# Two conditional residual layers: transposed operands from the host, a fused mask product, and layer 0 of batch b+1 ahead of layer 1 of batch b

## What is computed

```python
# per batch b of 8: x is 256x1024, mask 1024x1024 of 0/1, W0 and W1 1024x1024, A 1024x16, B 16x1024
y = x + (x @ W0.T + b0 + (x @ (2*mask[b] - 1)) * coeff[b])
z = y + (y @ W1.T + b1 + 2.0 * (y @ A[slot[b]]) @ B[slot[b]])
```

## Time and profile before

| what | us |
|---|---|
| device time, median of 3 runs | 426.68 |
| the three runs | 426.68, 426.79, 423.54 |
| span of the profiled execution | 421.9 |
| PE busy in it | 411.8 (98%) |
| DVE busy / ACT busy / POOL busy | 229.0 / 229.4 / 38.8 |
| first matmul of layer 0 | at 13.56 |
| first matmul of layer 0 of batch 1 | at 79.66 |
| last closing matmul's copy begins | at 419.07 |

### The profile page before, as it was taken

How to read it: one execution, slowest core, us unless ns; L and a number is a source line. 1 busy time by engine, 2 the same in 40 slices (tenths; PEclk the granted TensorE clock), 3 DMA queues, 4 the chain that set the end, 5 groups by cost and what they waited for, 6 DMA issues and landing times.

```text
span 421.9 us, 7924 instructions
## 1 busy us (share of the span) xinstructions
PE 411.8 (98%) x3034; PEld 408.3 (97%) x3034; DVE 229.0 (54%) x281; ACT 229.4 (54%) x371; POOL 38.8 (9%) x43
## 2 busy tenths in 40 slices
PE   6997999999999999999999999999999999999997
PEld 5897999999999999999999999999999999999996
DVE  1888786465536665374546755356653745365300
ACT  3775786664546465474547555363655735464311
POOL 1123530020000200020000200002000200002000
PEclk9999999999999999999999999999999999999999
DMA  7999735372146603292144712375142721440011
GB/s 227 341 332 322 254 153 197 105 230 101 50 151 178 251 5 139 74 309 101 50 149 128 246 55 61 138 230 198 49 125 93 260 99 50 149 132 0 2 50 51
DMA packets 34612, 61.56 MB, mean 146 GB/s; under 512 B 10652, under 2 KB 20004, under 8 KB 34598
## 3 DMA queue, kind: packets, MB, share of 16 engines
q1 hardware_dynamic: 31984, 52.96, 38.3%
q10 hardware_dynamic: 2614, 8.41, 5.6%
HBM read 52.97 MB, written 8.39 MB: 145 GB/s over the span
## 4 chain that ended last, share of the span: by engine, by line
PE 96%; DMA 1%; ACT 1%; issue 1%; POOL 0%; SPq 0%; ACTq 0%; POOLq 0%
PE y_ps L378 44%; PE z_ps L405 43%; PE z_ps L329 2%; PE z_ps L431 2%; PE t_ps L352 2%; DMA w_stage<-in_w 1%; PE y_ps L329 1%; PE z_ps L352 1%; PE y_ps L352 1%; ACT wc_hi L518 0%; PE y_ps L421 0%; PE y_ps L292 0%; ACT w_t L536 0%; PE t_ps L329 0%; POOL w_stage L247 0%
## 5 line engine op out<-in xcount | busy, mean ns | idle before, releaser
L378 PE MATMUL y_ps<-x_hi,wc_hi 128*128 128x256 f32 x512 | 143.0, 283 | 0.7 <-ACT wc_hi L518 0.7
L378 PE MATMUL y_ps<-x_lo,wc_hi 128*128 128x256 f32 x512 | 142.7, 283 | 0.0
L378 PE MATMUL y_ps<-x_hi,wc_lo 128*128 128x256 f32 x512 | 137.4, 284 | 0.0
L405 PE MATMUL z_ps<-w_hi,y_hi 128*128 128x344 f32 (+1 forms) x384 | 125.4, 327 | 0.0
L405 PE MATMUL z_ps<-w_lo,y_hi 128*128 128x344 f32 (+1 forms) x384 | 123.5, 322 | 0.0
L405 PE MATMUL z_ps<-w_hi,y_lo 128*128 128x344 f32 (+1 forms) x384 | 122.6, 319 | 0.0
L692 DVE TENSOR_TENSOR masks<-masks,w_t 128x1024 f32<-128x1024 f32 x64 | 90.4, 1413 | 43.6 <-ACT masks L511 42.8
L378 PEld LDWEIGHTS y_ps<-x_hi,wc_hi 128*128 128x128 f32 x512 | 98.1, 192 | 1.3 <-issue 0.7
L378 PEld LDWEIGHTS y_ps<-x_lo,wc_hi 128*128 128x128 f32 x512 | 98.2, 192 | 0.0
L378 PEld LDWEIGHTS y_ps<-x_hi,wc_lo 128*128 128x128 f32 x512 | 94.6, 192 | 0.0
L511 ACT ACTIVATE masks<-masks,coeff_now 128x1024 f32<-128x1024 int32 x64 | 79.4, 1243 | 16.5 <-DMA masks<-in_mask 10.1
(11 more groups left out here) (63 smaller groups left out, 221.9 us busy)
## 6 DMA issues: line engine op xcount, KB each, us to landing
masks<-in_mask SPq DMA_DIRECT2D x64, 512.0 KB, 4.4
out<-z_rows ACTq DMA_DIRECT2D x15, 512.0 KB, 4.0
x_rows<-in_x SPq DMA_DIRECT2D x7, 1024.0 KB, 5.3
w_stage<-in_w SPq DMA_DIRECT2D x6, 512.0 KB, 8.0
w_stage<-in_w SPq DMA_DIRECT2D x3, 1024.0 KB, 6.5
b_raw<-in_lora_b SPq DMA_DIRECT2D x32, 64.0 KB, 2.6
x_rows<-in_x SPq DMA_DIRECT2D x4, 256.0 KB, 6.7
z_rows<-in_w SPq DMA_DIRECT2D x2, 512.0 KB, 8.7
```

The lines of the kernel that those rows point to most:

```text
L378: ins = pe.matmul(y_ps[o // PAIR][:, (o % PAIR) * T:(o % PAIR + 1) * T], w[:, k % RING, o * P:(o + 1) * P], xs[:, k, :], start=(k == 0 and ...
L405: ins = pe.matmul(z_ps[g][:, 0:EDGES[g + 1] - EDGES[g]], ys[:, k, s * P:(s + 1) * P], w[:, k, EDGES[g]:EDGES[g + 1]], start=(k == 0 and n ...
```

## The change

The host hands over x as `x[b, p, k, t]`, W0 and W1 as `[k, p, o]`, A as `[slot, p, k, r]` and b0 as `[p, k]`, all transposed; all PE transposes but `turn_h` go, and so do the PSUM readers behind them. `signed_mask` and `set_coeff` go: DVE computes mask*2c + W0 in one `scalar_tensor_tensor` from the integer mask, ACT adds -c as it rounds the high part, and DVE adds it again for the low part. W1 comes through the mask ring, as its entries 16 to 23, after the masks of batches 0 and 1 (`w1_entry`). y has two buffers. PE does layer 0 of batch 0, then for b = 1 to 7 layer 0 of b and layer 1 of b-1, then layer 1 of batch 7. All loops are unrolled. Within a layer-0 block all sixteen high matmuls come before the eight low ones. Thirty warm-up transposes stand at the start.

```diff
+            for k in range(KT):          # SP
+                load_w0(k)
+                load_mask(0, k)
+                if k % PAIR == 0:
+                    load_x(0, k // PAIR)
+            for g in range(XG):
+                load_x(1, g)
+            for k in range(KT):
+                load_mask(1, k)
             sp.wait_ge(ids_in, 16)
             load_lora(0)
+            for k in range(KT):
+                load_w1(k)
+            for b in range(2, NB):
+                for g in range(XG):
+                    load_x(b, g)
+                for k in range(RING):
+                    load_mask(b, k)
+                load_lora(b - 1)
+                for k in range(RING, KT):
+                    load_mask(b, k)
             load_lora(NB - 1)
...
+            def ring_free(e):
+                e -= RING
+                if e < 0:
+                    return
+                if e < 2 * KT:
+                    sp.wait_ge(wc_lo_done, e + 1)
+                elif e < 3 * KT:
+                    sp.wait_ge(w1_lo_done, e - 2 * KT + 1)
+                else:
+                    sp.wait_ge(wc_lo_done, e - KT + 1)
...
+            for k in range(KT):          # POOL, after W0's diagonal and the b1 rows
+                e = w1_entry(k)
+                ring_filled(pool, e)
+                blk = sums[:, e % RING, k * P:(k + 1) * P]
+                pool.tensor_tensor(blk, blk, ident[:], ALU.add).then_inc(w1_diag, 1)
+            for b in range(NB):
                 lora_low(b)
...
+            def layer0_high(b, k):       # PE
+                pe.wait_ge(x_lo_done, XG * b + k // PAIR + 1)
+                pe.wait_ge(wc_hi_done, KT * b + k + 1)
+                for o in range(KT):
+                    if k == 0 and o % PAIR == 0:
+                        need(pe, y_lo_done, KT * (b - 1) + o + PAIR)
+                    ys = y_ps[o // PAIR][:, (o % PAIR) * T:(o % PAIR + 1) * T]
+                    w = wc_hi[:, k % RING, o * P:(o + 1) * P]
+                    for n in range(2):
+                        pe.matmul(ys, w, x_two[:, k, n, :], start=(k == 0 and o % PAIR == 0 and n == 0),
+                                  stop=False, skip_group_check=True)
...
+                    if b == 0 and s == 0 and g == 0:      # layer1_group
+                        pe.wait_ge(w1_lo_done, KT)
                     if s == 0 and g == 0:
                         pe.wait_ge(lora_lo_done, 2 * (b + 1))
+                        pe.wait_ge(y_lo_done, KT * (b + 1))
...
+            warm_up(30)
+            layer0(0)
+            for b in range(1, NB):
+                layer0(b)
+                layer1(b - 1)
+            layer1(NB - 1)
...
             def weights_high(b, k):      # ACT
                 act.wait_ge(sum_done, KT * b + k + 1)
                 block_read(act, b, k - RING)
-                act.activation(wc_hi[:, k % RING, :], sums[:, k % RING, :], ACT.Copy).then_inc(wc_hi_done, 1)
+                act.activation(wc_hi[:, k % RING, :], sums[:, mask_entry(b, k) % RING, :], ACT.Identity,
+                               bias=coeff_neg[:, b:b + 1]).then_inc(wc_hi_done, 1)
...
+            for k in range(KT):
+                if k % PAIR == 0:
+                    x_high(0, k // PAIR)
+                weights_high(0, k)
+            x_high(1, 0)
+            x_high(1, 1)
+            weights_high(1, 0)
+            weights_high(1, 1)
+            x_high(1, 2)
+            weights_high(1, 2)
+            act.wait_ge(b0_in, 16)
+            for g in range(XG):
+                y_high(0, g)
+            x_high(1, 3)
+            for k in range(3, 6):
+                weights_high(1, k)
+            w1_high(0)
+            weights_high(1, 6)
+            w1_high(1)
+            weights_high(1, 7)
+            for k in range(2, KT):
+                w1_high(k)
+            lora_high(0)
...
+            for a in (NB - 2, NB - 1):   # ACT, the end
+                for s in range(ST):
+                    h_high(a, s)
+                    h_copy(a, s)
+                    z_copy(a, s, 0)
+                    z_copy(a, s, 1)
+                    if a == NB - 1:
...
+                    else:
+                        z_copy(a, s, 2)
+                        store(a, s)
+                if a < NB - 1:
+                    lora_high(a + 1)
...
             def weights_sum(b, k):       # DVE
+                e = mask_entry(b, k)
+                ring_filled(dve, e)
+                if b == 0:
+                    dve.wait_ge(w0_diag, k + 1)
+                dve.scalar_tensor_tensor(out=sums[:, e % RING, :], in0=ring[:, e % RING, :],
+                                         scalar=coeff_two[:, b:b + 1], in1=w0_t[:, k, :],
+                                         op0=ALU.mult, op1=ALU.add).then_inc(sum_done, 1)
...
+            weights_sum(0, 0)
+            x_low(0, 0)
+            for k in range(KT - 1):
+                step(0, k)                       # weights_sum(0, k + 1), weights_low(0, k)
+                if k % PAIR == 0 and k < KT - PAIR:
+                    x_low(0, k // PAIR + 1)
+            weights_sum(1, 0)
+            weights_low(0, KT - 1)
+            x_low(1, 0)
+            x_low(1, 1)
+            step(1, 0)
+            step(1, 1)
+            x_low(1, 2)
+            step(1, 2)
+            dve.wait_ge(b0_in, 16)
+            for g in range(XG):
+                y_low(0, g)
+            x_low(1, 3)
+            for k in range(3, 6):
+                step(1, k)
+            w1_low(0)
+            step(1, 6)
+            w1_low(1)
+            step(1, 7)
+            for k in range(2, KT):
+                w1_low(k)
+            for b in range(2, NB):
+                a = b - 2
+                for g in range(XG):
+                    y_low(b - 1, g)
+                h_low(a, 0)
...
```

More of the change, by code:

```diff
@@ L383, in layer0_block, with layer0_low @@
+            def layer0_low(b, k):
+                pe.wait_ge(wc_lo_done, KT * b + k + 1)
+                for o in range(KT):
+                    ys = y_ps[o // PAIR][:, (o % PAIR) * T:(o % PAIR + 1) * T]
+                    w = wc_lo[:, k % RING, o * P:(o + 1) * P]
+                    ins = pe.matmul(ys, w, x_two[:, k, 0, :], start=False, stop=(k == KT - 1), skip_group_check=True)
+                    if k == KT - 1 and o % PAIR == PAIR - 1:
                         ins.then_inc(y_full, 1)
-                if k < KT - 1 and part != "high":
+                if k < KT - 1:
@@ L508, in signed_mask @@
-            def signed_mask(b, k):
-                act.wait_ge(mask_in[k % RING], 16 * (2 * b + k // RING + 1))
-                act.activation(sums[:, k % RING, :], masks[:, k % RING, :], ACT.Identity,
-                               bias=coeff_now[:, 1:2], scale=coeff_now[:, 0:1]).then_inc(signed_done, 1)
             def weights_high(b, k):
@@ L664, in _ @@
-            x_high(0, 0)
-            act.wait_ge(pairs_done, 2)
-            set_coeff(0)
-            w0_left_copy(0)
-            signed_mask(0, 0)
-            for j in range(2):
-                act.dma_start(b_raw[LR + j:LR + j + 1, :], b1.rearrange("(a n) -> a n", a=1)).then_inc(b1_in, 16)
-            act.wait_ge(b0_ps, 1)
-            act.activation(b0_cols[:], y_ps[0][:, 0:KT], ACT.Copy).then_inc(b0_done, 1)
-            act.wait_ge(b0_done, 1)
-            batch(0, first=True)
-            with act.Fori(1, NB - 1) as b:
-                batch(b)
@@ L678, in _ @@
-            batch(NB - 1, last=True)
+            act.dma_start(coeff_all[:], coeff).then_inc(coeff_in, 16)
+            act.dma_start(ids[:], slot_ids).then_inc(ids_in, 16)
+            act.dma_start(b0_cols[:], b0).then_inc(b0_in, 16)
+            for j in range(2):
+                act.dma_start(b_raw[LR + j:LR + j + 1, :], b1).then_inc(b1_in, 16)
+            act.wait_ge(ones_done, 1)
+            act.activation(h_rows[:, 0, 0:2], h_rows[:, 0, LR:KS].bitcast(F32), ACT.Identity).then_inc(table_used, 1)
@@ L789, in _ @@
-            dve.memset(h_rows[:, :, LR:KS].bitcast(F32), 1.0).then_inc(ones_done, 1)
-            x_low(0, 0)
-            w0_right_copy(0)
-            weights_sum(0, 0)
-            dve.wait_ge(b0_done, 1)
-            batch(0, first=True)
-            with dve.Fori(1, NB - 1) as b:
-                batch(b)
-            batch(NB - 1, last=True)
+            dve.memset(h_rows[:, :, LR:KS].bitcast(F32), 1.0).then_inc(ones_done, 1)
+            dve.wait_ge(coeff_done, 2)
+            weights_sum(0, 0)
@@ L801 @@
+            for g in range(XG):
+                y_low(NB - 1, g)
+            for a in (NB - 2, NB - 1):
+                for s in range(ST):
+                    h_low(a, s)
 def kernel(x, condB_coeff, itok_B_0_23, mask_Bx4096x4096_ik1, L0_cond_W, L0_cond_b, L1_cond_W, L1_cond_b,
```

564 lines of the change are left out of this document (147 added, 417 removed).

## The result

| kernel | median us | runs |
|---|---|---|
| before (same chip) | 425.37 | 4, 423.54 to 426.79 |
| changed | 430.47 | 4, 429.57 to 431.37 |

Ratio 1.0128, 95% interval 1.0093 to 1.0163: slower by 1.3%, some 5 us. The forecast was 425.3 us and its likeliest case no change; the time lies in the range, at its upper end, on the side to which the forecast gave the least chance. The profiled execution of the changed kernel took 429.57 us with a span of 427.8.

The account below looks back on a forecast made before the run. PE was taken to bound the kernel: 78.3 us to layer 1 of batch 0, then products 329.7, clock 3.6, adapter 6.0 and end 2.9 give a 420.5 us span; 4.8 above it, 425.3 us, range 419 to 431.

Parts of the forecast that it names:

- What bounds, products, the loop: Steady batches: PE alone sets their length, 46.97 us each without transposes instead of 48.73; all products 375.8 us.
- The start: Before layer 0 of batch 0: with no transposes ahead, the first product comes at 9.0 us instead of 13.56.
- Batch 0: Layer 0 of batch 0: batch 1's first mask is in at 31.9 us, and the layer ends at 35.3.
- Batch 1's layer 0: PE waits for DVE's first low part of y until 43.8 us, idling 8.5; the layer ends at 68.6.
- W1: W1's chain through the mask ring, landings of 3.5 us: layer 1 of batch 0 begins at 78.3, PE idling 9.7.
- rival B: W1's ring bounds: landings of 6.5 and diagonal adds of 1.4 us, 3.8 more per link, time 436.7; chance 0.07.
- Adapter of batch 7: Before layer 1 of batch 7: PE idles 6.0 us, as the single adapter buffer is freed only when batch 6 ends.
- The clock: After idle pauses PE runs at half clock; 1.8 us per return, charged 0.8, 1.8 and 1.8 after three pauses.
- Rival A: Short pauses: transfers at 413 GB/s, landings at 3.1 us, PE not slowed; time 418.3; chance 0.33.
- Fused pass: DVE's pass computing weights from the integer mask at 1024 columns: taken as 1.14 us, bounds 1.07 to 1.57.
- Rival C: Fused pass takes 1.57 us, so DVE sets the start: +8 us, time 433; chance 0.05.
- D: Unrolled code does not arrive in time, giving PE gaps in every batch; chance 0.03.

Follow-up runs that it names:

- e4: Changed kernel with POOL's passes over b1's rows moved behind the adapter's low part of batch 0: 427.78 us, ratio 1.0070.
- e15: e10 with batch 1's first mask asked for ahead of x blocks 2 and 3 of batch 1: 411.09 us, ratio 0.9670.
- e2: Changed kernel with y of batch 0 converted before the weight sums of batch 1's blocks 1 to 3: 434.02 us, ratio 1.0204.
- e13: e10 plus the edit of e2, y of batch 0 converted before the sums of batch 1: 412.06 us, ratio 0.9689.
- e5: Changed kernel with W1's blocks 0, 1, 6 and 7 loaded through the idle output buffer instead of the mask ring: 425.19 us, ratio 0.9992.
- e3: Changed kernel with the adapter's A part made early and its B part awaited only at the closing product: 421.51 us, ratio 0.9900.
- e8: Changed kernel with small groups of unneeded identity products on PE in its long pauses: 427.83 us, ratio 1.0074.
- e10: Changed kernel with the edits of e3, e4 and e5 together: 411.18 us, ratio 0.9672.
- e12: e11 with four more unneeded products after the first sum, before layer 0's first product: 413.06 us, ratio 0.9723.
- e11: e10 with small unneeded identity products on PE in the two remaining pauses: 414.78 us, ratio 0.9749.

## Why the prediction was wrong, step by step

- **What bounds, products, the loop**: right. 46.98 us a batch against 46.97; PE without a gap.
- **The start**: first product at 9.59 against 9.0. W0 and mask were in earlier than forecast, DVE's sum starting at 5.58, but x landed only at 7.77, and ACT rounds it before the weights. Half a microsecond, within its bounds.
- **Batch 0: the first failed step, a term put at nothing.** It had DVE start `weights_sum(1, 0)` at 31.9, when its mask is in, and took all work of DVE until then as hidden. It starts at 36.55. e4 divides the 4.65: 2.4 are POOL's b1 rows, 2.3 stay without them. The rows priced a collision of the port for the diagonals, and I quoted the rule, but I did not look for what else POOL would now do beside a busy DVE; in the kernel before, b1's rows stood behind W1's diagonals. Of the other 2.3, 1.42 are the wait for the mask in e4, which a steady stream of 395 GB/s had put at 31.9, and 0.9 DVE's own passes. What the mask's late landing costs in the time is not shown: e15 could win 0.8 us of it at most and is within the error.
- **Batch 1's layer 0**: the mechanism and the length were right. From the sum to the first `y_low` 11.4 us (36.55 to 47.93) against 11.0; PE resumes at 48.94 against 43.8. But e2 and e13 show that this pause hides behind the next one: shortened by 5.4 and 7.4 us, it gave nothing.
- **W1: the second failed step, by size.** From the end of the y passes to layer 1 were forecast 78.3 - 46.3 = 32.0 us and measured 85.63 - 51.1 = 34.5. Landings of 3.9, 3.3 and 3.7 against 3.5 and diagonal adds of 0.47, 0.58 and 0.51 against 0.6 are right, so rival B (landings of 6.5, adds of 1.4) did not occur. The low part of (1, 4) came 0.7 later, DVE waiting for ACT and ACT for PE at half clock, and the hop of block 0 took 7.7 instead of 6.4: 0.8 of it lies between DVE's last pass and the request (56.96 to 57.74), because SP was still issuing the first adapter's loads, which stand ahead of W1 in its queue and which the sum left out:

```profile
55.92 1.76 SPq L178 DMA_DIRECT2D b_raw<-in_lora_b  x4
```

At the other two links the request followed within 0.03 us. The last 0.5 us is in DVE's next four passes (4.9 against 4.6) and in the last hop. The prediction's own terms give 78.1 for layer 1, not 78.3. Its bound for transfers at 341 GB/s comes to +4.0 us, not +4.5. That the chain bounds is shown by e5.
- **Adapter of batch 7**: 4.75 against 6.0; ACT was free 0.5 us after PE's last product (393.85 to 394.31), not 1.7. Shown by e3. That the stretch after 85.63 came out as forecast is partly luck: this pause is 1.2 us shorter, the two slow returns cost 0.6 more, and products and end together 0.6 more.
- **The clock**: 1.9 and 2.3 us against 1.8 at the two returns that count. Shown by e8 and, for the last one, by e3. The Trainium skill, "TensorE: Matmul & The Clock Gate", section "HAM oscillation", has an idle stretch followed by half clock; these returns agree. Rival A took off 4.4 us for the clock where the sum holds only 3.6: the 0.8 after the first pause lies under W1's chain.
- **Fused pass**: pitch 1.20 us against 1.14. Rival C (1.57) did not occur; nor did D, as the loop shows no gap.
- **The distance to the median**: I added 4.8 us to the span because no time of the profiled execution was given. The changed kernel's is 1.8, and so is the kernel before's in every later run (423.28 with a span of 421.5); the other 3.0 are there because the profiled execution was one of the quicker ones. This hid 3 of the 7.3 us of the miss in the number, and it made the change look even: against 421.9 + 1.8 = 423.7 the forecast would still have been 1.4 better, and it came out 5.9 worse. So it is luck that the time lies in the range: with 1.8 the sum gives 422.3, and a range as wide around it ends at 428.

So: of the 7.3 us, 4.8 came from DVE being late with y, which W1's chain passed on, and 2.5 from that chain itself. Of the 4.8, the 2.4 of POOL's b1 rows are shown by e4; the other 2.4 and the division of the 2.5 are read from the traces and not tested apart.

## What to carry to other kernels

When an order is changed, list for every engine what it does beside the newly critical one, also the small preparatory operations that were harmless before: 2-partition copies on POOL cost DVE 3.7 us here. Where PE waits twice in a row for one engine's program, price only the last wait: work brought forward on that engine made the first wait 5.4 and 7.4 us shorter here and the time no better. List too what stands ahead of a critical load in its queue. The best version came from taking waits apart (A part and B part, ring and spare buffer), not from filling them. Where the code up to a step was the same, executions reached it up to 1.8 us apart, more than some of the effects sought.

## What the runs showed of the hardware

- POOL and DVE stretch each other: a copy of 2x1024 went from 1.03 us (e10) to 1.91, a subtraction from 2.37 to 3.25, and DVE's 1.27 to 2.05 and 3.41. The Trainium skill, "SBUF — State Buffer", section "SBUF: two separate sides", has the loser of the shared pair wait for the other's whole instruction; these rows agree: DVE's three passes end at 31.32, 34.66 and 36.63, each 1.1 us after POOL's, at 30.24, 33.57 and 35.55, as if each began its own work only then. They also show that even one or two partitions are enough.
- After pauses of 4.75 and 10.8 us the granted clock fell to 1.2 GHz, and 36 products of layer 1 took 8.03 and 7.58 us instead of 5.72; over the runs with such returns it was 7.4 to 8.7. After a pause of 2.6 us they took 7.55 in e10, and after one of 2.3 us 6.03 in e15, 0.3 more than at full speed. What decides it is not shown. Products put into a pause brought 2.6 us in e8 and lost 1.9 and 3.6 in e12 and e11, where they outlasted the pause.
- The clock at the start differs between profiled executions with the same 30 warm-up transposes: from 9 to 18 us 0.62 in e11, 0.81 in e5 and 1.00 in e10. Why is open, and so is whether the kernel or the execution decides it.
